# Candidate sums and rectified scores on GpSimd, shifted expert numbers, in an attention and expert-lookup kernel

## What is computed

```python
x = x + xattn(layernorm(x), ctx, ctx, Wq, bq, Wk, bk, Wv, bv, Wo, bo)      # 16 heads of 16
x = x + ffn(layernorm(x), norm_w, wq, keys, expert_down, expert_up)

def ffn(x, ...):                                 # HEADS 8, NUM_KEYS 64, K 16
    x_norm = x * rsqrt(mean(x * x) + EPS) * norm_w
    q = (x_norm @ wq).reshape(B, T, HEADS, 2, DIM_KEY)
    sim = einsum('bthpd,hkpd->pbthk', q, keys)
    s1, i1 = top_k(sim[0], K); s2, i2 = top_k(sim[1], K)
    all_idx = i1[..., :, None] * NUM_KEYS + i2[..., None, :]
    all_scores = s1[..., :, None] + s2[..., None, :]
    final_scores, pk = top_k(all_scores.reshape(.., K * K), K)
    final_idx = take_along_axis(all_idx.reshape(.., K * K), pk)
    hidden = gelu(einsum('btd,bthkd->bthk', x_norm, expert_down[final_idx])) * relu(final_scores)
    return einsum('bthk,bthkd->btd', hidden, expert_up[final_idx])
```

## Time and profile before

| what | us |
|---|---|
| median of 3 runs | 1328.29 |
| lowest and highest run | 1323.45, 1329.32 |
| time of the profiled execution | 1320.42 |
| its span, first to last instruction | 1318.6 |
| busy: PE, DVE, ACT, POOL | 1079.4, 1085.9, 395.0, 517.9 |
| mean granted share of TensorE's clock | 0.903 |

### The profile page before, as it was taken

How to read it: one execution, slowest core, us unless ns; L and a number is a source line. 1 busy time by engine, 2 the same in 40 slices (tenths; PEclk the granted TensorE clock), 3 DMA queues, 4 the chain that set the end, 5 groups by cost and what they waited for, 6 DMA issues and landing times.

```text
span 1318.6 us, 28688 instructions
## 1 busy us (share of the span) xinstructions
PE 1079.4 (82%) x10152; PEld 743.2 (56%) x10152; DVE 1085.9 (82%) x5027; ACT 395.0 (30%) x724; POOL 517.9 (39%) x467
## 2 busy tenths in 40 slices
PE   4799987796877762467897997989887989899998
PEld 2344433242223221356776876877776878778887
DVE  2667556979999998699999999999999999995621
ACT  1256554443434540121221222222221222222211
POOL 5230410502012012235646556565646564655500
PEclk9799998998778885658998999999998989999999
DMA  4344313222111101700000000010000010000000
GB/s 155 100 147 134 119 58 113 69 70 76 48 45 39 50 10 36 305 2 1 24 6 27 24 10 24 2 32 15 24 11 24 2 32 15 24 10 27 2 17 9
DMA packets 59925, 63.76 MB, mean 48 GB/s; under 512 B 6882, under 2 KB 56164, under 8 KB 59268
## 3 DMA queue, kind: packets, MB, share of 16 engines
q1 hardware_dynamic: 59780, 61.90, 14.4%
HBM read 42.21 MB, written 19.66 MB: 47 GB/s over the span
## 4 chain that ended last, share of the span: by engine, by line
DVE 47%; PE 36%; issue 6%; POOL 5%; DMA 3%; ACT 2%; SPq 2%; DVEq 0%; POOLq 0%; ACTq 0%; another core or an unknown queue 0%
PE bank L1229 34%; DVE mem L1186 6%; DVE mem L1152 4%; DVE mem L1199 4%; DVE mem L1018 3%; DVE mem L1019 3%; DVE mem L1183 2%; DVE mem L1087 2%; PE bank L1232 2%; DVE mem L1023 2%; DVE mem L1015 2%; DVE mem L1027 2%; DVE mem L1039 2%; DVE mem L1083 1%; DVE mem L1090 1%
## 5 line engine op out<-in xcount | busy, mean ns | idle before, releaser
L1229 PE MATMUL bank<-mem 128*128 128x32 bf16 (+5 forms) x9672 | 1030.7, 278 | 158.3 <-issue 66.6
L1229 PEld LDWEIGHTS bank<-mem 128*128 128x128 bf16 (+3 forms) x9672 | 691.0, 125 | 449.1 <-issue 211.9
L746 POOL TENSOR_TENSOR mem<-mem 128x1536 bf16<-128x1536 bf16 x118 | 330.9, 2805 | 291.2 <-DVE mem L1186 250.2
L1152 DVE TENSOR_REDUCE mem<-bank 128x1 f32<-128x512 f32 x256 | 167.5, 681 | 81.3 <-PE bank L1229 81.0
L845 ACT ACTIVATE mem<-bank 128x512 f32<-128x512 f32 x256 | 148.7, 601 | 209.6 <-PE bank L1229 208.8
L1199 DVE TENSOR_TENSOR mem<-mem 128x512 f32<-128x512 f32 x128 | 131.2, 1025 | 81.2 <-ACT mem L882 76.8
L882 ACT ACTIVATE mem<-bank 128x512 f32<-128x512 f32 x128 | 76.6, 598 | 342.4 <-PE bank L1229 342.4
L1186 DVE TENSOR_TENSOR mem<-mem 128x2048 bf16<-128x2048 bf16 x128 | 159.3, 1244 | 0.0
L1232 PE MATMUL bank<-mem 128*128 128x128 f32 (+3 forms) x480 | 75.4, 288 | 77.6 <-POOL mem L669 26.5
L891 ACT COPY mem<-bank 128x512 f32<-128x512 f32 x128 | 74.9, 586 | 167.2 <-PE bank L1229 167.2
L1232 PEld LDWEIGHTS bank<-mem 128*128 128x128 f32 (+3 forms) x480 | 54.9, 141 | 122.7 <-issue 95.3
(11 more groups left out here) (99 smaller groups left out, 749.8 us busy)
## 6 DMA issues: line engine op xcount, KB each, us to landing
mem<-parts_d SPq DMA_DIRECT2D x192, 64.0 KB, 2.3
parts_d<-mem SPq DMA_DIRECT2D x16, 384.0 KB, 2.6
mem<-in_L_ffn_expert_down SPq DMA_DIRECT2D x16, 256.0 KB, 2.9
downT_d<-mem SPq DMA_DIRECT2D x16, 256.0 KB, 3.1
mem<-downT_d SPq DMA_DIRECT2D x4, 1024.0 KB, 9.5
mem<-in_L_ffn_expert_up SPq DMA_DIRECT2D x4, 1024.0 KB, 17.3
tok_d<-mem SPq DMA_DIRECT2D x16, 160.0 KB, 1.8
mem<-tok_d SPq DMA_DIRECT2D x16, 160.0 KB, 2.4
```

Of the source, the lines that this page charges most:

```text
L746: nc.gpsimd.tensor_tensor(ow[q % 2], i0, i1, ALU.mult).then_inc(ow_rdy, 1)
L1152: nc.vector.tensor_reduce(nmx[g % 2][:, i % TB, i // TB:i // TB + 1], psum[n % 3][:, :], AX.X, ALU.max, negate=True).then_inc(s_max, 1)
L1229: return nc.tensor.matmul(o, l, r, start=first, stop=last)
```

## The change

The candidates' sums move from VectorE to GpSimd. `candidates(u)` on GpSimd takes the place of `candidate_numbers(u)`: seven float additions into `cand`, each of which reports by a new semaphore `cnd`; then one multiplication of all 256 indices of a token by 64 or 1, shifted left by LOW = 6 (`place_of`, into `iw`), seven integer additions into `cidx`, the addition of `pcode`, and as an instruction of its own the rectified scores (`wkey` = max(`cand`, 0)). `cix` now counts two per tile. GpSimd does this in the step of the eighth search, behind the `weigh` of that step. On VectorE the task `candidates` is empty, but there are two of it in `TASKS`, so that 19 entries and no longer 18 are spread over the same steps. `choose(v, 0)` waits for the seven `cnd` and then does a copy of one number. `make_keys` waits for `cix` and has four instructions with three operands in place of six. `decode` has one instruction less.

```diff
-        TASKS = ([("search", h) for h in range(FH)] + [("candidates", 0)] + [("choose", s) for s in range(4)] +
+        TASKS = ([("search", h) for h in range(FH)] + [("candidates", 0), ("candidates", 1)] + [("choose", s) for s in range(4)] +
                  [("keys", 0)] + [("extract", s) for s in range(4)])
...
-            def candidate_numbers(u):
+            def candidates(u):
 
                 at_least(pool, st1, (u + 1) * FH)
                 at_least(pool, key, u)
...
-                n0 = steps.count(nc.gpsimd.tensor_tensor(i64, ii[:, :, 0, :], k64.unsqueeze(2).to_broadcast([P, FH, TOPK]),
-                                                         ALU.mult))
+                for to, i0, i1 in each_segment(cand, s16[:, :, 0, :], s16[:, :, 1, :]):
+                    nc.gpsimd.tensor_tensor(to, i0, i1, ALU.add).then_inc(cnd, 1)
+                pool.wait_ge(cnd, (u + 1) * len(SEGS))
+                n0 = steps.count(nc.gpsimd.tensor_tensor(iw, i16, place_of.unsqueeze(1).unsqueeze(3)
+                                                         .to_broadcast([P, FH, 2, TOPK]), ALU.mult))
                 steps.after(n0)
...
+                for to, i0, i1 in each_segment(cidx, iw[:, :, 0, :], iw[:, :, 1, :]):
+                    steps.count(nc.gpsimd.tensor_tensor(to, i0, i1, ALU.add))
                 steps.all()
                 nc.gpsimd.tensor_tensor(cidx, cidx, pcode, ALU.add).then_inc(cix, 1)
+                nc.gpsimd.tensor_scalar(wkey, cand, 0.0, None, ALU.max).then_inc(cix, 1)
...
                 for q, k, par, kk, now in walk(*where):
-                    for tile, kind, i in now["tasks"]:
-                        if kind == "candidates":
-                            candidate_numbers(tile)
                     if on(kk, -1, 6) and not (kk == -1 and q in OWN):
                         weigh((k + 1) * 16 + q, par, q)
+                    for tile, kind, i in now["tasks"]:
+                        if (kind, i) == ("search", FH - 1):
+                            candidates(tile)
...
-            def choose(s):
+            def choose(v, s):
 
                 hs = (2 * s, 2 * s + 1)
                 if s == 0:
-                    steps.all()
+                    dve.wait_ge(cnd, (v + 1) * len(SEGS))
+                    nc.vector.tensor_copy(gate[:, 0:1], gate[:, 1:2])
...
-                relu = steps.count(nc.vector.tensor_scalar(wkey, cand, 0.0, 0.0, ALU.max, ALU.add))
-                steps.after(relu)
-                low = steps.count(nc.vector.tensor_scalar(ik, w, (1 << LOW) - 1, 12, ALU.bitwise_and,
-                                                          ALU.logical_shift_left))
+                dve.wait_ge(cix, 2 * (v + 1))
+                steps.all()
+                low = steps.count(nc.vector.scalar_tensor_tensor(ik, w, (1 << LOW) - 1, cidx, ALU.bitwise_and,
+                                                                 ALU.bitwise_or))
+                steps.after(low)
                 high = steps.count(nc.vector.scalar_tensor_tensor(w, w, LOW, pcode, ALU.logical_shift_right,
                                                                   ALU.bitwise_or))
-                dve.wait_ge(cix, v + 1)
-                steps.after(low)
-                nc.vector.tensor_tensor(ik, ik, cidx, ALU.bitwise_or).then_inc(key, 1)
+                nc.vector.scalar_tensor_tensor(ikey, c1, GONE, ikey, ALU.is_equal, ALU.mult).then_inc(key, 1)
                 steps.after(high)
+                dve.wait_ge(key, v + 1)
                 steps.count(nc.vector.scalar_tensor_tensor(wkey, c1, GONE, wkey, ALU.is_equal, ALU.mult))
-                dve.wait_ge(key, v + 1)
-                steps.count(nc.vector.scalar_tensor_tensor(ikey, c1, GONE, ikey, ALU.is_equal, ALU.mult))
...
-                wb = steps.count(nc.vector.tensor_scalar(wB, b, 12, (1 << LOW) - 1, ALU.logical_shift_right,
-                                                         ALU.bitwise_and))
...
-                nc.vector.tensor_tensor(bits(wf), wA, wB, ALU.bitwise_or).then_inc(dec_w, 1)
+                nc.vector.scalar_tensor_tensor(bits(wf), b, (1 << LOW) - 1, wA, ALU.bitwise_and, ALU.bitwise_or)\
+                  .then_inc(dec_w, 1)
```

53 lines of the change are left out of this document (23 added, 30 removed).

## The result

The changed kernel takes 1340.74 us (median of 4 runs, 1339.71 to 1344.87), the kernel before 1325.94 (median of 4 runs, 1323.45 to 1329.32): ratio 1.0107, 95% interval 1.0076 to 1.0138. It is slower, by 14.8 us on the medians. The forecast was 1333 with a range of 1313 to 1349, as the same within 0.5%. Between the two profiled executions the difference is larger, 1320.42 to 1340.72, so 20.3 us; that of before lay 5.5 us under its median, that of after on it.

What follows compares the result with a forecast made beforehand. VectorE was taken to set the pace up to about 1172 us. The terms -11 (attention), +20.2 (third steps) and -4.3 (given back later) summed to +5 us on the median 1328.29, so 1333, range 1313 to 1349.

Steps and rivals of the forecast that it cites:

- The third step: Expert stage, ten tiles: the third step behind the eighth search ends later as weightings wait behind GpSimd's chain, 20.2 us more.
- each 0.1 us of it is 1 us: Expert stage: how strongly the sum hangs on the length of GpSimd's chain, where each 0.1 us is 1 us in all.
- The chain: GpSimd's instructions from first sum to next product: 6.1 us undisturbed, 9.3 to 10.0 in most expert-stage tiles with VectorE's disturbance.
- Given back later: Expert stage, later in each tile: shorter keys and decode, less what the new spread of tasks costs, 4.3 us less.
- The attention: Attention, tiles 0 to 5: VectorE loses sums, key and decode instructions, 2.55 us per tile for tiles 0 to 3; 11 us less.
- (b): Expert stage: VectorE and GpSimd keep each other off for whole instructions, two sets cost 4.2 us, not 2.8; 1347 us, chance 0.26.
- (c): Attention gives nothing because TensorE or ScalarE is right behind VectorE there, so -11 falls away; 1344 us, chance 0.08.
- (d): Float additions are slow on GpSimd, 2.9 us undisturbed and not 1.8, 1.1 us per tile; 1344 us, chance 0.06.
- (a): Expert stage: the chain fits, only one set of VectorE's fixed work costs anything, 19 us less; 1314 us, chance 0.22.

Runs made afterwards that it cites:

- the kernel in pieces: The changed kernel with GpSimd's chain in the expert stage issued in three pieces behind the weightings of three steps in a row: 1327.95 us, ratio 1.0012.
- With TensorE relieved in both kernels: Both kernels with one of the three parts of the weights multiplied, 32 of 48 matmuls a step left out: 1317.12 us before, 1329.07 us changed.
- the mixed version: Tiles 0 to 5 as changed, 6 to 15 as with shifted numbers alone: 1314.63 us with tile 1's input load ahead of the stores, 1324.78 without.
- the kernel with shifted numbers alone: The kernel before with only the expert numbers kept shifted; sums and rectified scores stay on VectorE, the chain in its old place: 1331.99 us, ratio 1.0028.

## Why the prediction was right, and where it was not

**The third step, +20.2, measured +21.3.** The mechanism and the size held tile by tile: 20.7 for tiles 11 and 14 (20.4 predicted), 20.0 for 12 and 15 (20.0), 20.4 and 20.3 for 10 and 13 (20.4), 22.2 for 6 (22.0), 20.2 for 7 and 9 (19.9), 19.4 for 8, which was even. The slope came out at 0.8 to 1.0 us per us, near what "each 0.1 us of it is 1 us" says, and the kernel in pieces showed that for two thirds it is the block, not the work. In two of ten tiles, the worked-out tile 14 among them, VectorE stood at the hidden values' product and not at `oj`; it waits for the same late product, so the size held.

**The chain, 9.3 to 10.0, measured 8.8 to 10.3**, but with its parts wrong both ways, so that the agreement is partly luck. The sums were as taken (1.80 for 1.83). The seven sums of tile 14 took 4.96 us, 3.2 more than alone; the prediction had 3.2 too, but 2.8 of it for two sets of fixed work and 0.4 for a third line 1199. There was no third one: the two sets alone cost 3.2. The rectified scores took 1.20 us and not 0.5. I had priced them by a cast of 512 numbers, 0.61 to 0.64; the bound of 1.04, the two-input addition of 400 numbers, would have been nearer. The Trainium skill, GPSIMD Engine Reference, section 4.1 (Engine selection), calls one-input work on GpSimd roughly line-rate; this row disagrees, 400 numbers took 3.3 times VectorE's 0.36. The multiplication came out 0.1 us shorter than taken. Undisturbed the chain is 6.7 us and not 6.1; that missing 0.6 did not show because the 9.9 laid out for tile 14 was already 0.6 above its own parts, 6.1 + 3.2.

**Given back later, -4.3, measured +3.0.** This is the step that failed. VectorE had less to do there, about as counted (the changed kernel's keys take 4.8 us from the first to the end of the last in six tiles, as laid out, and 3.7 in four; 43.6 us over the ten tiles for 47.9 before). But the term assumed that behind the block VectorE is again the only bound. It isn't: TensorE had stood idle without the late product and worked off what had piled up, and VectorE then waited for `gelu` and the coefficients. With TensorE relieved in both kernels the rest came out at -3.3.

**The attention, -11.** In the slots it held: the four odd slots with tasks are 2.4 to 3.8 us shorter (2.55 predicted; the keys alone save 0.36 us a tile there, 2.34 for 2.70, and not 0.6). What I had not followed is the queue behind the chain: a GpSimd chain 3.4 us later, the splits, four stores on SyncE, a load, and TensorE's wait of 6.0 us in slot 10. That wait the prediction put at nothing. The prediction followed each wait to VectorE, but not GpSimd's list in slot 9. Of the 11 us 6 to 9 came through: 8.6 on the medians of these two kernels (539.7 to 531.1), some 6 over all kernels of the table.

**The total.** 1333 was 7.7 us low: 7.3 from the term that didn't come back, 2.4 from the attention as these two medians have it, 1.1 from the third steps, 0.3 from steps 0 to 15; against that stand 1.3 less behind step 112 and 2.4 by which the kernel before ran below the median that I added to. The 0.3 that the sum misses is rounding and the like. The time lies in the range, but not for the range's reasons: that reached up to 1349 for rival (b), and the single most likely outcome, the same within 0.5%, did not come; it is 1.1% slower. The 0.40 given to slower stood on (b), (c) and (d), and none of these is what happened. (b) asked for 4.2 us of disturbance by two sets, the sum for 2.8; it was 3.2. The Trainium skill, SBUF — State Buffer, section "SBUF: two separate sides", has the port pair that VectorE and GpSimd share as an exclusive lock for a whole instruction; the key instruction of 2.95 us agrees with it, the 3.2 us are less than the 4.2 of that rival. (a) wanted a chain that fits, (c) an attention that gives nothing, (d) float sums of 2.9 us: the rows have 9.8 us, some 6 to 9 us by the estimates above, and 1.80 us.

## What to carry to other kernels

When work moves to an engine with slack, look at what stands behind it in that engine's list, and spread it so that no piece is longer than the room of one step, here somewhere between 5 us, which left no wait, and 9: the same instructions cost 24 us as one block and 8 as three pieces. Judge each stage on its own, since the same edit can gain in one and lose in another, and the mixed version beats both. Take a stage's worth from more than one profile where its length differs from run to run. And don't count on time given back behind a stall until it is clear which engine has a backlog there.

## What the runs showed of the hardware

A `tensor_scalar` with one input on GpSimd, 400 float numbers, took 1.20 us, more than an integer addition of two inputs of 400 numbers (1.03) and twice a cast of 512 (0.61). In slot 10 of the attention the granted clock fell to half for some 17 us in five of the fourteen profiled kernels and not in the others, with the same instructions for TensorE there. In the kernel with shifted numbers alone it fell at 280.7 us, and TensorE had been busy for 2.88 of the 4 us ahead. In the kernel before it fell at 279.0, with 3.24 us busy in the 4 ahead, and came back at 282.5. TensorE was busy at half the clock in both. The first and then the second kernel, columns as in the earlier trace rows:

```profile
276.16:280.16 4.00, 2.88 (x14) 1.37 (x12) 0.69 (x1) 1.56 (x3) 0.00 (x0) 1.00 0.01 2
280.16:284.16 4.00, 4.00 (x10) 1.53 (x8) 0.00 (x0) 0.37 (x1) 0.00 (x0) 0.57 0.00 0
```

```profile
275.00:279.00 4.00, 3.24 (x12) 1.38 (x10) 0.69 (x1) 0.94 (x2) 0.00 (x0) 1.00 0.00 0
279.00:282.50 3.50, 3.34 (x10) 2.35 (x10) 1.28 (x3) 1.23 (x4) 0.00 (x0) 0.51 0.11 33
```

The half clock made the slot 8 to 9 us longer in two kernels of the old kind and some 5 us in three of the new. What decides it was not found.
